# Another order of turns, banks and late loads in the attention pass of a macaron block

## The reference

```python
x = x + 0.5 * slot_layer(layernorm(x))
x = x + attention(layernorm(x))
x = x + 0.5 * slot_layer(layernorm(x))

# slot_layer (4 sequences of 2048, 64 slots)
h = gelu(concat(x, mean slot) @ w1.T + b1); logits = h @ w2.T + b2
alpha = softmax over the 8 largest logits of a row, 0 elsewhere
slots = GRU cell(alpha.T @ x / sum of alpha, initial slots)
out = (alpha @ (slots @ wv.T + bv)) @ wo.T + bo

# attention: q, k (each head at length 1), v, sigmoid gates a and b per head
for each row: state = a * state + k (b * (v - state k)).T; y = state q
out = (rmsnorm(y) * silu(x @ Wg)) @ Wo
```

## Time and profile before

| what | value |
|---|---|
| runs | 2669.80, 2670.61, 2679.14 us; median 2670.61 |
| profiled execution | 2676.29 us, of it 2674.5 us span |
| granted clock of TensorE, mean | 0.975 of full speed |
| busy: PE, DVE, ACT, POOL | 94%, 68%, 39%, 51% |
| moved by DMA | 233.70 MB, of it 16.78 MB output |

### The profile page before, as it was taken

How to read it: one execution, slowest core, us unless ns; L and a number is a source line. 1 busy time by engine, 2 the same in 40 slices (tenths; PEclk the granted TensorE clock), 3 DMA queues, 4 the chain that set the end, 5 groups by cost and what they waited for, 6 DMA issues and landing times.

```text
span 2674.5 us, 117064 instructions
## 1 busy us (share of the span) xinstructions
PE 2524.0 (94%) x51035; PEld 1788.1 (67%) x51035; DVE 1821.2 (68%) x5308; ACT 1050.8 (39%) x1962; POOL 1357.9 (51%) x1895
## 2 busy tenths in 40 slices
PE   7999879999999999999999999999999999999768
PEld 6788546666666666666666666666666666666544
DVE  7778456777666776667676667777677767677626
ACT  5777323333333333333333333333333333333220
POOL 2222155555556655555566665555555555555410
PEclk9999989999999999999999999999999999999869
DMA  7334022222222222222222222222222222222278
GB/s 232 109 109 149 16 62 71 71 69 69 67 67 69 68 70 66 72 72 72 72 72 72 69 70 61 62 69 72 68 69 72 72 72 72 72 72 71 64 262 329
DMA packets 440719, 233.70 MB, mean 87 GB/s; under 512 B 352336, under 2 KB 368784, under 8 KB 440208
## 3 DMA queue, kind: packets, MB, share of 16 engines
q1 hardware_dynamic: 430992, 209.44, 28.7%
q10 hardware_dynamic: 9216, 16.78, 1.7%
HBM read 125.49 MB, written 74.97 MB: 75 GB/s over the span
## 4 chain that ended last, share of the span: by engine, by line
PE 78%; DVE 8%; issue 5%; POOL 4%; ACT 2%; SPq 1%; DMA 1%; POOLq 0%; DVEq 0%; ACTq 0%
PE psum L881 26%; PE psum L936 8%; PE psum L1060 8%; PE psum L1078 5%; PE psum L1041 4%; PE psum L1021 3%; PE psum L988 3%; PE psum L1028 3%; PE psum L727 3%; PE psum L790 2%; PE psum L972 1%; PE psum L953 1%; PE psum L872 1%; POOL dm L2107 1%; PE psum L1098 1%
## 5 line engine op out<-in xcount | busy, mean ns | idle before, releaser
L881 PE MATMUL psum<-w_all,xnT 128*128 128x512 f32 (+2 forms) x2048 | 740.1, 502 | 1.9 <-ACT xnT L1687 1.4
L2036 POOL TENSOR_TENSOR sm<-sm,half 128x1 f32<-128x1 f32 (+1 forms) x384 | 536.4, 1397 | 70.3 <-ACT sm L1731 54.2
L881 PEld LDWEIGHTS psum<-w_all,xnT 128*128 128x128 f32 x2048 | 366.5, 191 | 219.3 <-issue 169.1
L2610 DVE TENSOR_TENSOR blk<-blk 128x30 f32<-128x30 f32 (+14 forms) x960 | 327.5, 341 | 73.7 <-issue 47.1
L2612 DVE TENSOR_TENSOR blk<-blk 128x30 f32<-128x30 f32 (+14 forms) x960 | 323.8, 337 | 33.0
L2068 POOL TENSOR_SCALAR sm<-sm 128x1 f32<-128x1 f32 x64 | 22.5, 351 | 557.6 <-DVE sm L2516 557.6
L936 PEld LDWEIGHTS psum<-xnT,w_all 128*128 128x128 f32 x2048 | 245.0, 194 | 58.1 <-issue 49.2
L936 PE MATMUL psum<-xnT,w_all 128*128 128x128 f32 x2048 | 275.4, 285 | 0.8 <-issue 0.6
L1060 PE MATMUL psum<-w_out,gate 128*128 128x512 f32 x512 | 259.5, 621 | 0.1
L1041 PE MATMUL psum<-qg,st 32*32 32x64 f32 x8192 | 175.1, 220 | 25.9 <-DVE st L2629 13.2
L1041 PEld LDWEIGHTS psum<-qg,st 32*32 32x32 f32 x8192 | 133.6, 106 | 68.2 <-DVE st L2629 39.3
(11 more groups left out here) (287 smaller groups left out, 4594.1 us busy)
## 6 DMA issues: line engine op xcount, KB each, us to landing
blk<-n_scratch SPq DMA_DIRECT2D x64, 512.0 KB, 4.0
xin<-in_L_attn_x_dram SPq DMA_DIRECT2D x96, 256.0 KB, 2.8
n_scratch<-nn SPq DMA_DIRECT2D x64, 256.0 KB, 4.3
xh<-xc SPq DMA_DIRECT2D x64, 256.0 KB, 2.6
e_scratch<-blk SPq DMA_DIRECT2D x32, 512.0 KB, 2.8
x_scratch<-xh SPq DMA_DIRECT2D x62, 256.0 KB, 2.6
rxn<-in_L_attn_x_dram SPq DMA_DIRECT2D x32, 256.0 KB, 3.2
pk<-kdt SPq DMA_DIRECT2D x128, 64.0 KB, 2.2
```

The lines of the kernel that those rows point to most:

```text
L881: last = mm(dst, xnT[b][:, k * P:(k + 1) * P], w_all[:, k * WK + at:k * WK + at + n], start=(k == 0), stop=(k == KC - 1))
L2036: return g.tensor_tensor(dst, a, half[:, 0:n], ALU.pow)
L2610: own(tt(o, Y[:, 0:rows, s_:s_ + 1].to_broadcast([P, rows, cols]), N[:, s_:s_ + 1, s_ + 1:CH].to_broadcast([P, rows, cols]), ALU.mult))
```

## The change

The attention pass gets a second order of its middle turns and its own lists for the first and the last turns, on all engines. The table of banks is new, and with it the waits in `free`. `fill`, a number of products on unneeded data at the start, goes from 55 to 43. In `step_pe`, `proj_va(q, 1, 0)` moves from a turn's end to its begin, `gram(q, 0, *)` and the parts of `apply_gy(r, 0, *)` mix, both `dec` stand between pieces of chain, `gram(q, 1, *)` behind `chain(r, 0, 3)`, and `hidden` later. In `step_act`, `gate_of(q, 1)` stands between `last_gelu(r, 0)` and `last_gelu(r, 1)`, which moved into the next turn, and `gates_exp(q)` behind that. In `first_dve`, sums and moments of tile 2 stand ahead of the inversion. At the end, `early_loads` is gone: two pairs are loaded behind `projected()`, four more once the chains of batch 0 have ended, and the cell's weights behind `store_alpha(NT - 1)`. The core of the diff:

```diff
-        ffn_at = [banks(1, 1), banks(3, 1)]
-        xT_at = [banks(0, 1), banks(6, 1)]
-        k_at = [banks(0, 1), banks(3, 1)]
-        q_at = [banks(2, 1), banks(1, 1)]
-        va_at = [banks(7, 1), banks(1, 1)]
-        vb_at = [banks(5, 1), banks(2, 1)]
-        g_at = [banks(2, 1), banks(5, 1)]
-        dec_at = [banks(0, 1), banks(4, 1)]
-        ones_at = [banks(5, 1)[:, 0:1], banks(6, 1)[:, 0:1]]
-        wo_at = [banks(2, 1), banks(7, 1)]
-        rxT_at = [banks(3, 1), banks(6, 1)]
-        h_at = [banks(1, 1), banks(3, 1)]
-        lg_at = [banks(1, 1)[:, 0:NS], banks(1, 1)[:, 0:NS]]
-        y_at = [banks(5, 2), banks(6, 2)]
-        cum_at = banks(6, 1)[:, 0:8 * H]
-        aT_at = banks(6, 1)[:, 0:P]
+        ffn_at = [banks(4, 1), banks(5, 1)]
+        xT_at = [banks(1, 1), banks(3, 1)]
+        k_at = [banks(2, 1), banks(5, 1)]
+        q_at = [banks(1, 1), banks(2, 1)]
+        va_at = [banks(6, 1), banks(3, 1)]
+        vb_at = [banks(7, 1), banks(1, 1)]
+        g_at = [banks(2, 1), banks(3, 1)]
+        dec_at = [banks(5, 1), banks(5, 1)]
+        ones_at = [banks(3, 1)[:, 0:1], banks(6, 1)[:, 0:1]]
+        wo_at = [banks(2, 1), banks(0, 1)]
+        rxT_at = [banks(4, 1), banks(3, 1)]
+        h_at = [banks(4, 1), banks(5, 1)]
+        lg_at = [banks(0, 1)[:, 0:NS], banks(2, 1)[:, 0:NS]]
+        y_at = [banks(6, 2), banks(6, 2)]
+        cum_at = banks(5, 1)[:, 0:8 * H]
+        aT_at = banks(4, 1)[:, 0:P]
         slot_at = banks(2, 1)
-        gram_at = [[banks(2, 1), banks(7, 1)], [banks(0, 1), banks(4, 1)]]
-        uw_at = [[banks(6, 1), banks(4, 1)], [banks(3, 1), banks(7, 1)]]
-        gq_at = [[banks(4, 1), banks(0, 1)], [banks(3, 1), banks(1, 1)]]
+        gram_at = [[banks(1, 1), banks(3, 1)], [banks(0, 1), banks(4, 1)]]
+        uw_at = [[banks(2, 1), banks(7, 1)], [banks(6, 1), banks(7, 1)]]
+        gq_at = [[banks(4, 1), banks(0, 1)], [banks(5, 1), banks(3, 1)]]

         block = ctx.enter_context(nc.Block())
...
+            def loads(first, last):
+                for i in range(first, last):
+                    x2_load(i)
+
+            def projected():
                 for name in ("k_ps", "q_ps", "va_ps", "vb_ps", "g_ps"):
                     sp.wait_ge(S[name], both(NT, 1))
+
+            def sums_done():
                 for b in range(B):
                     sp.wait_ge(hold_in[b], 16 * NT)
                 for name in ("xn", "ssq", "d33"):
                     sp.wait_ge(S[name], both(NT, 1))
-                for i in range(N_EARLY):
-                    if i == N_EARLY - 2:
-                        sp.wait_ge(e_out, 16 * NT)
-                    x2_load(i)
-
-            def drain_loads():
-                for b in range(B):
-                    sp.wait_ge(y1_turn[b], NC * NT)
-                for g in range(3):
-                    at_load(g)
-                for b in range(B):
-                    sp.wait_ge(ch_ps[b], NC * NT)
+                sp.wait_ge(e_out, 16 * NT)
+
+            def reload_cell():
                 n = 0
                 for buf, cols in wih_region:
                     sp.dma_start(buf[:, :], wih_dram[:, n * D:(n + cols) * D]).then_inc(wih_in, 16)
                     n += cols
                 for k in range(KC):
                     sp.dma_start(voT_at(k), vo_dram[:, k * D:(k + 1) * D]).then_inc(wih_in, 16)
+
+            def drain_loads():
+                sp.wait_ge(ch_ps[0], NC * NT)
+                sums_done()
+                loads(N_W, N_W + 4)
+                store_alpha(NT - 1)
+                for b in range(B):
+                    sp.wait_ge(y1_turn[b], NC * NT)
+                sp.wait_ge(ch_ps[1], NC * NT)
+                reload_cell()
+                loads(N_W + 4, N_EARLY)
+                for g in range(3):
+                    at_load(g)
                 sp.wait_ge(S["wo_ps"], both(NT, 1))
                 sp.wait_ge(S["ones_ps"], both(NT, 1))
-                for i in range(N_EARLY, N_DRAIN):
-                    x2_load(i)
+                loads(N_EARLY, N_DRAIN)

...
                 inverse_in(NT, 1)
-                key_across(NT, 1)
+                projected()
+                loads(0, N_W)
                 store_alpha(NT - 2)
                 drain_loads()
                 store_second(NT, 0)
                 store_second(NT, 1)
-                store_alpha(NT - 1)
                 store_alpha(NT)

             def first_sp():
...
                 pe.wait_ge(S["rhsd"], both(n, b))
+                if b == 0:
+                    free((n, (S["kn"], both(n, 1))))
+                else:
+                    free((n, (S["draw"], both(n, 0))))
                 for part, mask in enumerate((after, cross)):
...
                     pe.wait_ge(S["qt"], both(n, b))
-                    if b == 1:
-                        free((n, (S["draw"], both(n, 0))))
-                    if b == 1:
-                        free((n, (S["draw"], both(n, 1))))
+                    if b == 0:
+                        free((n, (S["va"], both(n, 1))))
+                    else:
+                        free((n - 3, (aT, n - 3 + NT)), (n - 1, (T["qg"][0], nth(n - 1, 0))), (n, (S["x1"], both(n, 0))))
...
             def step_pe(p, q, r, s, u):
+                proj_va(q, 1, 0)
                 proj_va(q, 1, 1)
                 apply_uw(r, 0, 0)
                 apply_uw(r, 0, 1)
@@ -1497,93 +1515,92 @@
                 apply_uw(r, 0, 3)
                 proj_k(q, 1, 0)
                 proj_k(q, 1, 1)
-                qe_T(r, 0, 0)
-                qe_T(r, 0, 1)
                 apply_gy(r, 0, 0)
+                proj_k(q, 1, 2)
+                proj_k(q, 1, 3)
+                proj_q(q, 1, 0)
                 apply_gy(r, 0, 1)
+                gram(q, 0, 0)
                 apply_gy(r, 0, 2)
-                proj_k(q, 1, 2)
-                proj_q(q, 1, 0)
-                proj_k(q, 1, 3)
+                gram(q, 0, 1)
+                apply_gy(r, 0, 3)
                 proj_q(q, 1, 1)
-                apply_gy(r, 0, 3)
                 proj_q(q, 1, 2)
                 proj_q(q, 1, 3)
-                gram(q, 0, 0)
+                gram(q, 0, 2)
+                gram(q, 0, 3)
                 chain(r, 0, 0)
-                gram(q, 0, 1)
+                alpha_T(u)
                 chain(r, 0, 1)
-                gram(q, 0, 2)
+                dec(q, 0)
                 chain(r, 0, 2)
-                dec(q, 0)
+                dec(q, 1)
                 chain(r, 0, 3)
-                gram(q, 0, 3)
-                dec(q, 1)
                 gram(q, 1, 0)
                 gram(q, 1, 1)
                 gram(q, 1, 2)
                 gram(q, 1, 3)
+                cum(q)
                 logits(s, 1)
-                cum(q)
-                out_proj(r, 0, 0)
-                out_proj(r, 0, 1)
+                qe_T(r, 1, 0)
+                proj_vb(q, 1, 0)
                 apply_uw(r, 1, 0)
                 apply_uw(r, 1, 1)
                 apply_uw(r, 1, 2)
                 apply_uw(r, 1, 3)
+                out_proj(r, 0, 0)
+                y_norm(r, 0)
+                out_proj(r, 0, 1)
+                qe_T(r, 1, 1)
                 out_proj(r, 0, 2)
-                qe_T(r, 1, 0)
-                qe_T(r, 1, 1)
-                y_norm(r, 0)
                 out_proj(r, 0, 3)
                 apply_gy(r, 1, 0)
+                slots(s)
                 apply_gy(r, 1, 1)
-                slots(s)
-                proj_g(q, 1, 0)
                 proj_g(q, 0, 0)
                 apply_gy(r, 1, 2)
                 apply_gy(r, 1, 3)
                 proj_g(q, 0, 1)
+                proj_g(q, 0, 2)
+                chain(r, 1, 0)
+                proj_g(q, 1, 0)
+                chain(r, 1, 1)
+                proj_vb(q, 1, 1)
+                chain(r, 1, 2)
+                ffn(p)
                 proj_g(q, 1, 1)
-                proj_g(q, 1, 2)
-                chain(r, 1, 0)
+                chain(r, 1, 3)
+                proj_g(q, 0, 3)
                 last_xT(r, 0)
-                chain(r, 1, 1)
-                proj_g(q, 0, 2)
-                ffn(p)
-                proj_g(q, 0, 3)
-                chain(r, 1, 2)
-                proj_g(q, 1, 3)
-                chain(r, 1, 3)
-                hidden(r, 0, 0)
-                proj_vb(q, 1, 0)
-                first_xT(p, 0)
-                hidden(r, 0, 1)
-                proj_k(p, 0, 0)
                 out_proj(r, 1, 0)
                 out_proj(r, 1, 1)
+                out_proj(r, 1, 2)
                 y_norm(r, 1)
-                out_proj(r, 1, 2)
                 out_proj(r, 1, 3)
-                alpha_T(s)
+                first_xT(p, 0)
+                proj_g(q, 1, 2)
+                proj_vb(p, 0, 0)
...
                 last_gelu(NT, 1)
                 last_exp(NT, 0)
+                last_aT(NT - 1)
                 last_exp(NT, 1)
                 slot_copy(NT)
...
             def step_act(p, q, r, s, u):
...
+                gate_of(q, 0)
```

(43 more changed lines are left out.)

925 lines of the change are left out of this document (467 added, 458 removed).

## The result

| | before | after |
|---|---|---|
| median of the runs | 2670.2 us | 2794.1 us |
| range | 2663.7 to 2679.1 (4 runs) | 2787.6 to 2798.2 (4 runs) |
| span of the profiled execution | 2674.5 us | 2789.5 us |
| product `ffn(4)` | 505.4 us | 502.4 us |
| `ffn(32)` | 2440.1 us | 2545.2 us |

The ratio is 1.0459, 95% interval 1.0421 to 1.0497. The forecast was 2681 us, with 2705 as the upper end. Of the 115 us between the two spans, 108 lie in the 28 middle turns (72.96 us each instead of 69.10), -3 in the first ones, and +10 at the end.

What follows compares the result with a forecast made beforehand. TensorE, busy 94% of the span, was taken as the bound, with stores bounding the last pass. First turns -5, middle +5.6, last turn -10, reload +20 sum to +10.6 us: 2681 us, range 2654 to 2705.

Steps and rivals of the forecast that it cites:

- (g): Middle turns: weight loads starting late where 32-row products are dense stay at 0.80 us a turn; bounds -0.5 and +0.6 us.
- (a) to (f): Middle turn: effects of new order, banks, waits and table loads; together +0.2 us a turn, bounds -0.8 and +0.8 us.
- (a): Middle turn: gram(q, 1, 0), now behind chain(r, 0, 3) in banks decay no longer uses, loses 0.84 us of waiting.
- rival 2: Middle turns: new 1 us wait each, from the table load through key and query transposes to gram(q, 0, 0); 2704 us; chance 0.17.
- (b): Middle turn: decay 1 must wait until decay 0 is evacuated, as both use bank 5; 0.25 us added.
- (c): Middle turn: the VectorE round trip from chain 0 to chain 1 stays, with less work covering it; 0.15 us added.
- my own case: Whole kernel: the main forecast, +0.2 us a middle turn and 2681 us in all; 2668 to 2694 us had chance 0.40.
- rival 1: Middle turns: 1 us shorter each, as waits are covered and late starts shrink; 2648 us; chance 0.21.
- (f): Middle turn: two more ScalarE table loads, 2 x 1.28 us, delay the gates; costed at nothing, uncovered up to 1 us.
- The first turns: Start: sums and moments fill VectorE's idle time, so tile 2's inverse comes earlier; -5 us, bounds -1 and -9.
- The last turn: Last turn: later sum and moments -1.6 us, two stops beside full DMA engines gone -5.9, earlier out_proj -2.7; -10 in all.
- The reload and the last pass: End: reload of the cell's weights waits behind the last exponential, delaying all transfers queued after it; +20 us, bounds +13 and +24.

Runs made afterwards that it cites:

- experiment 6: The kernel before with only the change's places of the last-pass loads; store_alpha(NT - 1) behind the ten pairs: 2677.0 us; straight behind the reload: 2671.4 us.
- the fastest kernel: The changed kernel with fill(61), store_alpha(NT - 1) behind reload_cell(), and alpha's transpose and copy earlier in the last lists: 2651.0 us, ratio 0.9929.

## Why the prediction was wrong

- **The step that failed is (g), the late starts.** It took the late starts of the earlier trace rows to belong to dense stretches and to stay what they were, 0.80 us a turn, with +0.6 us as the bound. They belong to the borders of blocks of 256 instructions. Stops at borders were 93.2 us over 27 turns instead of 11.2, 3.0 us a turn more (before, they were 0.4 us of the 0.80). With them came the half clock, of which the prediction has no term for the middle turns: 44.4 us instead of 6.8, by the estimate 0.7 us a turn (line 895's mean product took 511 ns instead of 500, 64 of them a turn). The other idle stretches shrank by 0.3 us a turn. That accounts for 3.4 of the 3.9 us a turn; the runs don't show where the last 0.5 lies. The shortest middle turn was 71.3 us, so the prediction's own sign of being wrong (over 0.8 us from 68.3) was there.
- **What should have been costed and wasn't** is `fill(55)` to `fill(43)`, together with the first lists. The prediction doesn't name it. It moved the borders by 48 instructions; in the kernel before, that alone costs 172 us, and in the changed kernel 18 products more give back 126.
- **The terms (a) to (f)** gave +0.2 us a turn. With the borders at a good place the new order's turn is 68.35 to 68.63 us against 69.10 us before and 68.88 with `fill(119)`: about -0.5 us. The waits did shrink, but (a) came only in part: of the 0.84 us that were to go ahead of `gram(q, 1, 0)`, 0.46 stayed, now for VectorE's transpose of the queries, a wait that no term had and that is near to rival 2's path. (b) showed 0.20 us where 0.25 was taken, and (c) fell to 0.17 instead of staying at 0.40. The result of this part lies between my own case and rival 1 (-1 us, decides from -0.6). (f): seven table loads stand in the turn from 2035.33, as predicted, and no stop of TensorE names ScalarE's gates.
- **The first turns** gave -3 us where -5 was said. The first correction came 10.9 us earlier (385.82, in the earlier trace rows 396.75), not 3, and `ffn(3)` came 10.9 us earlier too (425.93, in the earlier trace rows 436.78). The turn behind it, 76.5 us long instead of 68.6, gave 7.9 of that back, with 5.3 us of stops at borders where before there were none.
- **The last turn** was worth -11.5 us up to the exponential; -10 was said. The reason was wrong. The -5.9 us of stops did not come: up to the exponential, stops at borders were 10.3 us after and 6.5 before. Two of 2.26 and 3.10 us without a releaser are still there, the first beside idle DMA engines (share 0.00), the second beside full ones (0.96). With the old order and the loads moved away (experiment 6), one of 2.77 us was left beside a share of 0.29, and the other had shrunk to 0.28; and in the fastest kernel one of 4.16 us stands beside a share of 0.26. So full DMA engines are not needed for such a stop; whether they lengthen one isn't shown. What did shrink is the waits away from the borders (23.1 to 14.3 us) and the time at half clock (55.9 to 23.9 us); how they share in the -11.5 stays open. The same section of the Trainium skill that the prediction cites (Runtime: NRT & Kernel Launch, Instruction fetch mechanics) also gives the size of a block, 16 KiB or 256 instructions. The traces agree: 16.4 KB a packet, stops 256 instructions apart. Its sentence that the cost of crossing a border is mostly hidden holds here for the long blocks (0.05 us in the mean behind those of 3.6 to 4.0 us) and not for the short ones (1.9 us behind those of 1.4 to 1.6 us).
- **The reload and the last pass** were right: issued 0.95 us behind the last exponential, first products of the cell 15.4 us behind it (12 to 15 said), the end 96.9 us behind it (95.4 said), +21.4 us (+20 said).

So the sum was -5 + 5.6 - 10 + 20 and came out as -3 + 108 - 11.5 + 21.4 = 115 us.

## What to carry to other kernels

When a stop on TensorE names no releaser, number the recorded instructions and look at the numbers modulo 256 before blaming what stands there. Look at the granted clock behind such stops too. In a kernel with stretches of small products, any edit that changes how many instructions run ahead of a repeated list moves every border in it, so compare two orders only with a few such shifts of each; here a shift was worth up to 172 us and the order itself some 15. And before a store is moved in a queue, ask which engine waits for its landing ahead of its next stage.

## What the runs showed of the hardware

- TensorE's instructions arrive in blocks of 256, 16.4 KB a packet (6.59 MB in 402). A block that ran in 1.4 to 1.6 us was followed by 1.9 us of stop in the mean (41 blocks, 0.3 to 2.5 us). No block of the middle turns of any trace began less than 2.15 us after its packet had started.
- The same instructions in the same order took 69.2 to 79.2 us a turn, by the place of the borders and the half clock that comes with their stops.
- In the changed kernel each of the 11 half-clock stretches of the middle turns began beside a stop at a border, and so did the other 92 of all traces. With `fill(43)` on the kernel before, the clock was at half for 174.1 of 2084.8 us, with `fill(119)` in none of the middle turns. Stops at borders without such a stretch are common too (17 of the 28 turns of the changed kernel); what decides stays open.
- At a border, the packet for the next block started between 0.1 us before and 1.9 us after the block began (the twelve borders of one turn of the trace after, by the packets' start times), and at the five borders with a stop the next block started 2.2 to 2.7 us after its packet. What makes the first of these times so different stays open; so does a rule exact enough to give a turn's length for a border that hasn't been measured. My own, from block lengths alone, missed by up to 150 us.
